# Three narrow attentions: scores from bf16 parts over 64 rows a head, laid out by copies on the chip

## What is computed

```python
x = x + jnp.tanh(g_xattn[i]) * attention(_layernorm(x), ctx)
# attention, a head of 8 channels:
scores = q @ k.T / sqrt(8)          # 128 x 128 for each of 16 heads and 32 batches
probs = softmax(scores + mask)      # layer 0: key mask; layer 2: pair mask, 27 queries kept a head
out = (probs @ v, heads joined) @ Wo.T + bo
```

## Time and profile before

| | us |
|---|---|
| median of 3 runs | 1828.62 (1827.49 to 1828.67) |
| the profiled execution | 1831.42 |
| its span, first to last instruction | 1829.5 |
| attention 0, from 16.9 | 216.2 |
| attention 2, from 954.7 | 252.6 |
| attention 3, from 1490.8 | 213.4 |
| TensorE busy in the whole span | 1712.9 (94%) |
| VectorE, ScalarE, GpSimd busy | 1096.6, 872.4, 640.2 |

### The profile page before, as it was taken

One profiled execution on the slowest core, in us unless ns is written; L12 is line 12 of the kernel. 1 busy time (PEld: TensorE's weight loads), 2 busy tenths in 40 slices (PEclk: granted clock), 3 DMA queues, 4 the chain that ended last, 5 costly groups with the idle time before them and its releaser, 6 DMA issues. The chain is left out here.

```text
span 1829.5 us, 46859 instructions
## 1 busy us (share of the span) xinstructions
PE 1712.9 (94%) x17896; PEld 1094.6 (60%) x17896; DVE 1096.6 (60%) x2372; ACT 872.4 (48%) x2183; POOL 640.2 (35%) x1075
## 2 busy tenths in 40 slices
PE   4999989899999999878978999979999989999898
PEld 2555554577777777656665444446777765555454
DVE  5677767566666666553176777762222336777676
ACT  3555526456555555535344444434433336454354
POOL 4466508233232322302011455500000004666673
PEclk9999989999999999999998999979999999999999
DMA  5000041000000000010000000000000010000000
GB/s 115 2 3 3 2 118 35 9 7 8 5 8 7 5 8 4 2 47 23 23 28 24 3 3 3 3 1 0 1 0 0 0 35 13 2 3 2 2 24 23
DMA packets 47823, 27.66 MB, mean 15 GB/s; under 512 B 11024, under 2 KB 44560, under 8 KB 47632
## 3 DMA queue, kind: packets, MB, share of 16 engines
q1 hardware_dynamic: 42896, 24.64, 4.9%
q10 hardware_dynamic: 4736, 0.35, 0.2%
HBM read 22.88 MB, written 2.10 MB: 14 GB/s over the span
## 5 line engine op out<-in xcount | busy, mean ns | idle before, releaser
L837 DVE TENSOR_REDUCE neg_max<-scores 128x8 f32<-128x1024 f32 x192 | 235.0, 1224 | 131.9 <-PE scores L579 45.9
L1911 POOL TENSOR_TENSOR probs<-probs,inverse 128x512 f32<-128x512 f32 x128 | 133.3, 1041 | 322.8 <-DVE inverse L2115 322.8
L547 PE MATMUL scores<-k_diag,q_all 32*128 32x512 f32 x768 | 217.0, 642 | 6.5 <-ACT k_all L706 4.4
L561 PE MATMUL turned<-q_diag,k_all 32*128 32x512 f32 x768 | 216.4, 637 | 0.5 <-ACT probs L748 0.5
L748 ACT ACTIVATE probs<-turned 128x1024 bf16<-128x1024 f32 (+1 forms) x128 | 131.2, 1025 | 172.5 <-PE turned L593 172.5
L432 POOL TENSOR_TENSOR k_diag<-k_all,hmask 128x512 f32<-128x512 f32 x96 | 100.0, 1043 | 323.2 <-ACT k_all L706 293.9
L2049 ACT ACTIVATE probs<-scores,neg_max 128x128 f32<-128x128 f32 x512 | 180.8, 387 | 5.3 <-DVE neg_max L2107 5.3
L1569 ACT ACTIVATE hidden_f<-hb_f,b_f 128x512 f32<-128x512 f32 x128 | 88.1, 688 | 129.7 <-PE hb_f L1515 129.5
L1524 PEld LDWEIGHTS yb_f<-w_f,hidden_f 128*128 128x128 f32 x1024 | 119.2, 192 | 14.8 <-issue 14.8
L2040 ACT ACTIVATE heads_t<-heads 128x512 f32<-128x512 f32 x64 | 38.3, 598 | 173.3 <-PE heads L1976 173.3
L1524 PE MATMUL yb_f<-w_f,hidden_f 128*128 128x128 f32 x1024 | 119.3, 275 | 0.0
(11 more groups left out here) (326 smaller groups left out, 3744.2 us busy)
## 6 DMA issues: line engine op xcount, KB each, us to landing
ctx_t<-in_ctx_t_dram SPq DMA_DIRECT2D x24, 256.0 KB, 3.3
w_f<-in_L_ffn_W_dram SPq DMA_DIRECT2D x16, 256.0 KB, 3.2
x_state<-in_x_dram SPq DMA_DIRECT2D x4, 512.0 KB, 8.0
ctx_t<-in_ctx_t_dram SPq DMA_DIRECT2D x16, 128.0 KB, 2.1
out_dram<-x_state SPq DMA_DIRECT2D x7, 256.0 KB, 2.3
w_f<-in_L_ffn_We_dram SPq DMA_DIRECT2D x1, 1024.0 KB, 6.4
taps_f<-in_L_ffn_conv_w_dram SPq DMA_DIRECT2D x1, 768.0 KB, 6.3
y_weights_or_value_parts<-_ffn_expert_weights_dram SPq DMA_DIRECT2D x1, 512.0 KB, 4.4
```

The source lines that it names most:

```text
L547: last = nc.tensor.matmul(scores[pair][:, (g % 2) * 512:(g % 2 + 1) * 512], cols(q_all, b, S)[quad_rows(g), :], k_diag[quad_rows(g), b % 2 ...
L561: nc.tensor.matmul(turned[:, (g % 2) * 512:(g % 2 + 1) * 512], cols(k_all, b, S)[quad_rows(g), :], q_diag[quad_rows(g), b % 2, :, :].rearr ...
L837: v.tensor_reduce(neg_max[:, b % 2, 8 * pair:8 * pair + 8], scores[pair][:, :].rearrange("p (h k) -> p h k", k=S), axis=X_AXIS, op=ALU.max ...
L1911: nc.gpsimd.tensor_tensor(p4, p4, inverse[:, n % 2, CH * h:CH * h + CH].unsqueeze(2).to_broadcast([P, CH, S]), ALU.mult).then_inc(s["prob_ ...
```

## The change

Queries and keys are no longer multiplied in fp32. Each group's 128 x 512 queries (and keys) are split in three bf16 parts, high, middle and low: ScalarE casts (`high_of`, `mid_of`), GpSimd, or VectorE for the queries of layers 0 and 3's first two groups, subtracts (`rest_of`, `low_of`). The products of parts that are kept are eight (`Q_SLOTS`, `K_SLOTS`), so a head of 8 channels becomes 64 rows. A transfer for each slot copies one part on the chip into `q_rep` and `k_rep` (16 partitions x 8 KB, pieces of 1 KB): 16 transfers of 128 KB a group, issued by SP, four of them for group 0 by ScalarE. `q_rep` and `k_rep` are rings of three groups; the third place of each lies in memory of weights that are idle at the time, which is why the conv layer's weights are now loaded at the start of stage 5.

A pair's direct or crosswise scores are now eight bf16 matmuls of 64 rows x 128 columns (`score_heads`), in turn from the upper and the lower half of the rows, each with its own weights. `k_diag`, `q_diag`, `keys_apart`, `queries_apart` and the head masks are gone. The columns of Wq, bq, Wk and bk are put in another order (`BY_TILE`).

`q_all`, `k_all` and `v_all` are rings too, so the fills are spread over the loop: for group c, k in step 4c-10, t and q in step 4c-9, v in step 4c-7. TensorE waits for a group's 16 copies at its first batch. The context is loaded behind the copies of a group on SP. `load_later_stages` ends ahead of `load_conv`; the selection's scratch tiles move.

```diff
-    st.conv = dict(w1=sb("w1_f3", [P, 512]), w2=sb("w2_f3", [P, 512]), taps=sb("taps_f3", [P, 3, 512]),
-                   conv_b=sb("conv_b_f3", [P, 512]),
-                   w_tap=sb("w_tap_f3", [P, 3, 512]), w2_int=sb("w2_int_f3", [P, 4, D], BF16),
+    spare = sb("conv_weights_or_copies", [P, 8 * 512])
+    st.early_spare = shared[:, 0:8 * 512].bitcast(BF16).rearrange("p (n k c) -> p n k c", n=2, k=8)
+    st.conv_spare = spare[:, :].bitcast(BF16).rearrange("p (n k c) -> p n k c", n=2, k=8)
+    st.conv = dict(w1=spare[:, 0:512], w2=spare[:, 512:1024], taps=spare[:, 1024:2560].rearrange("p (k h) -> p k h", k=3),
+                   conv_b=sb("conv_b_f3", [P, 512]), w_tap=spare[:, 2560:4096].rearrange("p (k h) -> p k h", k=3),
...
+Q_SLOTS = (0, 0, 1, 1, 0, 2, 1, 2)
+K_SLOTS = (0, 1, 0, 1, 2, 0, 2, 1)
+SLOTS = len(Q_SLOTS)
+COPIED = 16 * SLOTS
+RING = 3
 
 
 def attention_small(nc, st, arg, layer, mask=None, select=False):
 
     GW = GB * S
-    KV0, TQ0 = (4, NG) if select else (EARLY, 1)
+    KV0, TQ0 = (3, NG) if select else (EARLY, 2)
...
-        q_all, k_all, v_all = sb("q_all", [P, NB * S]), sb("k_all", [P, NB * S]), sb("v_all", [P, NB * D])
-        k_diag, q_diag = sb("k_diag", [P, 2, 4, S]), sb("q_diag", [P, 2, 4, S])
+        CR = 3 if select else 4
+        ctx_t, xn, xn_t = sb("ctx_t", [P, CR, GW]), sb("xn", [P, 2, GW]), sb("xn_t", [P, 2, GW])
+        QR, VR = NG if select else 2, 3
+        q_all, k_all, v_all = sb("q_all", [P, QR * GW]), sb("k_all", [P, KV0 * GW]), sb("v_all", [P, VR * GW])
+        q_parts, k_parts = (sb(n, [P, 2, 3, GW], BF16) for n in ("q_parts", "k_parts"))
+        spare = st.early_spare if layer == 3 else st.conv_spare
+        q_rep, k_rep = ([sb(f"{n}{i}", [P, 8, GW], BF16) for i in range(RING - 1)] + [spare[:, i, :, :]]
+                        for i, n in enumerate(("q_rep", "k_rep")))
...
+        fill_at = {}
+        for c in range(NG):
+            if c >= TQ0:
+                fill_at.setdefault((4 * c - 9, 0), []).append(("t", c))
+                fill_at.setdefault((4 * c - 9, 1), []).append(("q", c))
+            if c >= KV0:
+                fill_at.setdefault((4 * c - 10, 0), []).append(("k", c))
+                fill_at.setdefault((4 * c - 7, 1), []).append(("v", c))
+
         def first_fills(b):
-
-            return [("t", c) for c in [b + AHEAD + 1] if TQ0 <= c < NG] + [("k", c) for c in [b + AHEAD + KV0] if KV0 <= c < NG]
+            return fill_at.get((b, 0), [])
...
+        def made_by(kind, b, half):
+
+            early = KV0 if kind in "kv" else TQ0
+            return early + sum(k == kind for (step, part), todo in fill_at.items() if (step, part) <= (b, half) for k, _ in todo)
...
+            def load_context(c):
+                wait(sp, s["v_done"], c - CR + 1)
+                sp.dma_start(ctx_t[:, c % CR, :].rearrange("p (b k) -> p b k", b=GB),
+                             arg["ctx_t"][c * GB:(c + 1) * GB].rearrange("b d k -> d b k")).then_inc(ctx_in[c % CR], 16)
+
+            def replicate_keys(c):
+                sp.wait_ge(s["k_low"], c + 1)
+                for slot, part in enumerate(K_SLOTS):
+                    sp.dma_start(k_rep[c % RING][slot:P:SLOTS, :, :], k_parts[:, c % 2, part, :]).then_inc(k_copied[c % RING], 16)
+
+            def replicate_queries(c, slots):
+                sp.wait_ge(s["q_low"], c + 1)
+                for slot in slots:
+                    sp.dma_start(q_rep[c % RING][slot:P:SLOTS, :, :], q_parts[:, c % 2, Q_SLOTS[slot], :]) \
+                        .then_inc(q_copied[c % RING], 16)
+
+            for c in range(CR):
+                load_context(c)
+            replicate_keys(0)
+            replicate_queries(0, range(SLOTS // 2))
+            for c in range(1, NG):
+                wait(sp, s["st_done"], 8 * (c - 2))
+                replicate_keys(c)
+                replicate_queries(c, range(SLOTS))
+                if c + CR - 1 < NG:
+                    load_context(c + CR - 1)
...
-            def keys_apart(b):
-                pool.wait_ge(s["k_ready"], b // GB + 1)
-                wait(pool, s["s1_done"], b - 1)
-                p.tensor_tensor(k_diag[:, b % 2, :, :], cols(k_all, b, S).unsqueeze(1).to_broadcast([P, 4, S]),
-                                st.hmask4[:, :].unsqueeze(2).to_broadcast([P, 4, S]), ALU.mult).then_inc(s["kdiag_ready"], 1)
-
-            def queries_apart(b):
-                pool.wait_ge(s["q_ready"], b // GB + 1)
-                wait(pool, s["st_done"], 2 * b - 2)
-                p.tensor_tensor(q_diag[:, b % 2, :, :], cols(q_all, b, S).unsqueeze(1).to_broadcast([P, 4, S]),
-                                st.hmask4[:, :].unsqueeze(2).to_broadcast([P, 4, S]), ALU.mult).then_inc(s["qdiag_ready"], 1)
+            def rest_of(name, u, whole, parts):
+                pool.wait_ge(s[name + "_high"], u + 1)
+                p.tensor_tensor(unit(whole, u), unit(whole, u), parts[:, u % 2, 0, :], ALU.subtract).then_inc(s[name + "_rest"], 1)
+
+            def low_of(name, u, whole, parts):
+                pool.wait_ge(s[name + "_mid"], u + 1)
+                p.tensor_tensor(parts[:, u % 2, 2, :], unit(whole, u), parts[:, u % 2, 1, :], ALU.subtract).then_inc(s[name + "_low"], 1)
...
+            for c in range(2):
+                rest_of("k", c, k_all, k_parts)
+                low_of("k", c, k_all, k_parts)
+                if select:
+                    rest_of("q", c, q_all, q_parts)
+                    low_of("q", c, q_all, q_parts)
+
             for b in range(-AHEAD - 1, NB):
                 if real(b + 1):
                     split_max(b + 1)
-                if real(b + AHEAD + 1):
-                    keys_apart(b + AHEAD + 1)
-                if real(b + 2):
-                    queries_apart(b + 2)
                 if real(b + 1) and not select:
                     values_apart(b + 1)
+                if 2 <= (b + 9) // 4 < NG and (b + 9) % 4 == 0:
+                    rest_of("k", (b + 9) // 4, k_all, k_parts)
+                if 2 <= (b + 8) // 4 < NG and (b + 8) % 4 == 0:
+                    low_of("k", (b + 8) // 4, k_all, k_parts)
+                    rest_of("q", (b + 8) // 4, q_all, q_parts)
+                if 2 <= (b + 7) // 4 < NG and (b + 7) % 4 == 0:
+                    low_of("q", (b + 7) // 4, q_all, q_parts)
...
+            def score_heads(to, still, moving, b, pair, stop):
+
+                at = slice(b % GB * S, b % GB * S + S)
+                still, moving = still[b // GB % RING], moving[b // GB % RING]
+                for j in range(4):
+                    for half in range(2):
+                        rows = slice(64 * half, 64 * half + 64)
+                        last = nc.tensor.matmul(to[:, half * 512 + j * S:half * 512 + (j + 1) * S],
+                                                still[rows, 4 * pair + j, at], moving[rows, 4 * pair + j, at],
+                                                start=j == 0, stop=stop, skip_group_check=True)
+                return last
+
             def direct(b, pair):
 
                 if not real(b):
                     return
                 if pair == 0:
-                    pe.wait_ge(s["kdiag_ready"], b + 1)
-                    pe.wait_ge(s["q_ready"], max(min(b + 1, NG), TQ0))
-                    pe.wait_ge(s["v_ready"], min(b + KV0, NG))
+                    if b % GB == 0:
+                        pe.wait_ge(k_copied[b // GB % RING], COPIED * (b // GB // RING + 1))
+                        pe.wait_ge(q_copied[b // GB % RING], COPIED * (b // GB // RING + 1))
+                    pe.wait_ge(s["q_ready"], made_by("q", b - AHEAD - 1, 1))
+                    pe.wait_ge(s["v_ready"], made_by("v", b - AHEAD - 1, 1))
                     if select:
                         topk["ranks_read"](pe, b - AHEAD)
                 else:
-                    pe.wait_ge(s["xnt_done"], max(min(b + 2, NG), TQ0))
-                    pe.wait_ge(s["k_ready"], min(b + 1 + KV0, NG))
+                    pe.wait_ge(s["xnt_done"], made_by("t", b - AHEAD, 0))
+                    pe.wait_ge(s["k_ready"], made_by("k", b - AHEAD, 0))
                     if select:
                         topk["ties_read"](pe, b - AHEAD)
                 wait(pe, max_done[pair], b)
-                for g in (2 * pair, 2 * pair + 1):
-                    last = nc.tensor.matmul(scores[pair][:, (g % 2) * 512:(g % 2 + 1) * 512], cols(q_all, b, S)[quad_rows(g), :],
-                                            k_diag[quad_rows(g), b % 2, :, :].rearrange("p h k -> p (h k)"),
-                                            start=True, stop=mask is None, skip_group_check=tiled)
+                last = score_heads(scores[pair], q_rep, k_rep, b, pair, mask is None)
...
-                if pair == 0:
-                    pe.wait_ge(s["qdiag_ready"], b + 1)
                 wait(pe, s["exp_done"], 2 * b + pair)
-                for g in (2 * pair, 2 * pair + 1):
```

(51 more changed lines are left out.)

91 lines of the change are left out of this document (49 added, 42 removed).

## The result

The changed kernel takes 1797.27 us as a median of 4 runs (1795.33 to 1803.66), against 1828.05 for the kernel before beside it: a ratio of 0.983 (95% interval 0.9814 to 0.9846), -31 us. Forecast were 1790 and -38. The profiled execution took 1795.33, with a span of 1793.5.

What follows compares the result with a forecast made beforehand. TensorE was taken to bound layers 0 and 3, a chain through the buffer `turned` layer 2. Loops -4.8, -21.6, -5.8 and starts -7, +1 summed to -38: 1793 us profiled, 1790 as a median, range 1762 to 1835.

Steps and rivals of the forecast that it cites:

- Scores: Score matmuls of a half step on TensorE: 0.55 us against 0.98, halves overlapping, with 0.10 for a layout change.
- The new wait: Shifts in layers 0 and 3 wait 0.2 us for ScalarE's copy of the turned maxima; a batch takes 4.70.
- Fills: Later groups' projections inside the loops: waits charged at 0.9 us a group in layer 3, 1.3 in layer 0, 0.3 in layer 2.
- Loops: First to last reciprocal of the narrow attentions: layer 0 168.2 us (-4.8), layer 2 162.0 (-21.6), layer 3 166.2 (-5.8).
- the selection's second half: Eights, ties and ranks on VectorE in layer 2's loop, estimated to add 9 us.
- Copies: On-chip copies, 2 MB a group: 7 us of SP's issuing and 7.6 of transfer, hidden in the loop, costing 0.
- Starts: Start of each attention: first scores some 7.5 us later; net 0 in layer 0, +1 in layer 3, -7 in layer 2.
- a sign of being wrong: At the attention starts: a first exponential later than 10 us after that of the kernel before would show the forecast wrong.
- Rival (a): Layers 0 and 3 give nothing because VectorE and ScalarE couple in every step: about -18, 1811 us; chance 0.20.
- (b): Shifts' or fills' wait hardly shows, 4.45 us a batch, first reciprocals 3 us earlier: 27 more gained, 1765; chance 0.10.
- (c): The 64-row halves of the score matmuls do not overlap, 5.39 us a batch in layers 0 and 3: +24, 1853; chance 0.12.
- (d): Copies come late, a group's 2 MB taking over 18.8 us; at 25, +140 less the gain; chance 0.05, shared with another rival.

Runs made afterwards that it cites:

- the spread kernel: Kernel after, with the four tiles VectorE normalises for a later group done one a step instead of all in one step: 1790.69 us, ratio 0.9791.
- the idle matmuls: Kernel after, with 44 idle fp32 matmuls added in layers 0 and 3 and 28 in layer 2 where TensorE stands: 1794.16 us, ratio 0.9805.

## Why the prediction held, point by point

- **Scores.** 0.55 a half step forecast and found, and the overlap of the halves priced by itself (+71 us without it). This step carried the forecast. The Trainium skill's page TensorEngine Tiling (Array Packing), section Tiling Modes, says that tiles operate independently; the runs agree, with the order of issue free as well. It says too that a change of tiling mode drains TensorE: sixteen matmuls at 0.24 for eight are 0.48, so 0.07 is left before the shifts, where my sum had 0.45 and 0.10.
- **The new wait.** 0.2 forecast and found, with a plain batch at 4.72 against 4.70. In layer 2 4.64 against 4.66.
- **Fills.** A group costs 4.7 in layer 0 and 4.3 in layer 3 more than four plain batches, as charged, and the spread kernel shows the cause of 0.85 of it to be the one named.
- **Loops.** 168.6 against a forecast of 168.2, and 166.5 against 166.2. Layer 2: 156.8 against 162.0, 5.2 better. Four terms make it up. Plain batches are 4.64 instead of 4.66 (0.6). A group's keys and values cost 1.95, not 2.2, so the wait of 0.3 that I charged is not there (five groups, 1.2). The last three steps are 3.2 shorter than plain ones, not 2.5 (0.7). What is left, above all the selection's second half, is 6.4 instead of my 9, the largest miss of the four (2.6): 156.8 less 31 x 4.64 and 5 x 1.95, plus 3.2.
- **Copies.** Hidden in the loop, as said, at 271 GB/s against the 275 used. But "7 us of SP" was 12: an issue costs 0.63 and more, where I had taken 0.44 from key masks. It is SP's time, and not the 7.6 us of transfer, that makes the margin in the loop thin: twice the issues cost 56 us.
- **Starts.** This is the step that failed, in each layer in the same direction. The first reciprocals came 2.6 and 2.0 later in layers 0 and 3, not 0 and 1, and 4.0 earlier in layer 2, not 7: 6.6 in all. In layers 0 and 3 the miss lies ahead of the first scores, which came 9.4 later in both, not 7.5. The term that was too small is the four issues behind the queries' low part. I had 1.8 us for them; in layer 3 the low part is there at 1471.9, SP issues keys until 1473.05 and its own four until 1475.8, 3.9 in all. The landing behind it, 3.6 to 3.7, is inside my 3 to 4. Whether cheaper issues would have brought the scores forward is open, since the DMA engines are full in that stretch; the sum had neither the keys' row on SP nor the 2 MB as a whole, which take 11.4 us there and not 7.6. The first exponential came 9.7 later in layer 3, not 8.7, and 10.0 in layer 0, at the edge of what I had named as a sign of being wrong. The granted clock behind TensorE's stand was in no step of the sum either; its price is not shown. In layer 2 the 3 us that are missing have no cause yet: neither SP issuing all eight copies (61.2 against 61.5) nor the idle matmuls (63.4) brought them back.
- **The rest.** Stages that the change does not touch differ by +3.0 (wide), +1.8 (capacity), +1.2 (convolution), -4.5 (gelu) and -1.7 (linear), -0.2 in all. Their work is the same; the windows give the wide attention 0.99 of the clock against 1.00, gelu 0.97 against 0.95. In two of the four kernels with idle matmuls the wide attention took 463.7 again. What decides the clock there was not tried.

The sum as profiled: -4.4 - 26.8 - 5.5 for the loops, +2.6 - 4.0 + 2.0 for the starts, -36.1, against -38. That the two lie so close is in part luck: the loops gave 4.5 us more than forecast and the starts 6.6 less. As medians it is -31, since the profiled execution of the kernel after is 1.9 below its median, the fastest of its four, and that of the kernel before 3.4 above its own. Rival (a), the coupling, has no sign in the plain steps; (b) did not come, because 0.2 of wait and VectorE's normalising are both there; (c) and (d) were real prices, and the kernel stands on the right side of both.
